# Second FFN of a gated two-layer block: the expert weights of gate and up become the stationary operand, and the second product follows one tile behind

## What is computed

```python
router_logits = jnp.einsum('sbh,eh->sbe', hidden_states, router_w)
routing_indices = jnp.argmax(router_logits, axis=-1)
out = jnp.zeros_like(hidden_states)
for e in range(E):                                   # E = 8, I = 352, H = 128
    mask = (routing_indices == e)[..., None]
    xe = jnp.where(mask, hidden_states, 0.0)
    g = jnp.einsum('sbh,ih->sbi', xe, gate_w[e])
    u = jnp.einsum('sbh,ih->sbi', xe, up_w[e])
    ye = jnp.einsum('sbi,hi->sbh', jax.nn.silu(g) * u, down_w[e])
    out = out + jnp.where(mask, ye, 0.0)
...
x = x + jnp.tanh(g_ffn[1]) * _L1_ffn_ref(_layernorm(x, axis=-1), ...)
```

## Time and profile before

| what | value |
| --- | --- |
| median of 3 runs | 825.99 us (825.89 to 826.08) |
| span of the profiled execution, first to last instruction | 815.2 us |
| around the span (median less span) | 10.8 us |
| mean granted TensorE clock | 0.995 |
| PE busy over the span | 775.3 us, 95% |
| PEld, DVE, ACT, POOL busy | 78%, 76%, 68%, 58% |
| second FFN, from its first instructions to the end of the span | 717.8 to 815.2 us |
| its first products of steps 1 to 12 begin | 729.13 us (step 1) to 797.46 us (step 12) |

### The profile page before, as it was taken

The page is one execution under the profiler, slowest core; times in us unless marked ns, Lnnn a source line. Parts: engine busy times, 40 slices in busy tenths (PEclk is TensorE's granted clock), DMA queues, the critical chain, the costliest instruction groups (busy, mean ns, idle before and its releaser), DMA issues. The chain is left out here.

```text
span 815.2 us, 30741 instructions
## 1 busy us (share of the span) xinstructions
PE 775.3 (95%) x10664; PEld 637.5 (78%) x10669; DVE 622.4 (76%) x2406; ACT 558.0 (68%) x1125; POOL 476.5 (58%) x892
## 2 busy tenths in 40 slices
PE   4999999999999989999999999999999999889995
PEld 2777877787788868888888888888888888558884
DVE  4799999998677767888888888888888888734442
ACT  1688878886455568777777777777777777447762
POOL 6645777773011156577677686676776776605554
PEclk9999999999999999999999999999999999999998
DMA  8804999800200000000000000000000000023110
GB/s 223 303 3 149 264 241 235 195 1 3 72 1 0 0 1 2 3 7 7 7 0 7 7 7 7 7 0 7 7 7 7 0 7 7 10 68 91 33 33 19
DMA packets 56157, 41.65 MB, mean 51 GB/s; under 512 B 3897, under 2 KB 51651, under 8 KB 55856
## 3 DMA queue, kind: packets, MB, share of 16 engines
q1 hardware_dynamic: 52400, 36.39, 17.8%
q0 software_dynamic: 2272, 4.27, 1.6%
q10 hardware_dynamic: 1440, 0.40, 0.4%
HBM read 18.07 MB, written 23.44 MB: 51 GB/s over the span
## 5 line engine op out<-in xcount | busy, mean ns | idle before, releaser
L1654 PE MATMUL l_pv<-l_Z,l_probs 128*128 128x129 f32 x1024 | 164.1, 284 | 0.6 <-DVE l_acc L1161 0.6
L1654 PEld LDWEIGHTS l_pv<-l_Z,l_probs 128*128 128x128 f32 x1024 | 138.4, 191 | 20.0 <-DVE l_acc L1161 4.9
L1433 POOL TENSOR_TENSOR l_qk_lo<-w,l_qk_hi 128x512 f16<-128x512 f32 x132 | 148.9, 1160 | 1.7 <-ACT l_qk_hi L1511 1.3
L1161 DVE SCALAR_TENSOR_TENSOR x_sb<-l_pv,l_inv,x_sb 128x128 f32 (+1 forms) x256 | 89.8, 351 | 35.3 <-DVE l_inv L1148 6.9
L52 PE MATMUL l_tz<-M,cT 128*128 128x512 f16 x396 | 108.0, 382 | 0.2 <-DVE l_Z L1239 0.2
L1497 ACT ACTIVATE l_probs<-l_b 128x512 f32<-128x512 f32 x128 | 72.8, 594 | 50.5 <-PE l_b L1620 50.4
L1487 ACT ACTIVATE w<-l_qk_bank 128x512 f32<-128x512 f32 x129 | 77.0, 597 | 44.1 <-PE l_qk_bank L52 42.4
L520 DVE TENSOR_REDUCE n_shared<-fold_bank 128x4 f32<-128x512 f32 x128 | 87.3, 682 | 9.5 <-PE fold_bank L735 9.3
L1138 DVE TENSOR_REDUCE l_neg_max<-l_a 128x4 f32<-128x512 f32 x132 | 85.8, 681 | 2.6 <-PE l_a L1598 2.1
L1491 ACT ACTIVATE l_qk_hi<-w 128x512 f16<-128x512 f32 x129 | 80.5, 624 | 1.1
L1502 ACT ACTIVATE l_Z<-l_tz 128x512 f32<-128x512 f32 x128 | 76.7, 599 | 3.6
(11 more groups left out here) (291 smaller groups left out, 2266.4 us busy)
## 6 DMA issues: line engine op xcount, KB each, us to landing
expert_rows<-empty_row SPq DMA_DIRECT2D x8, 2178.0 KB, 24.6
x_sb<-expert_rows SPq DMA_DIRECT2D x36, 66.0 KB, 2.1
x_sb<-in_x SPq DMA_DIRECT2D x4, 512.0 KB, 6.9
ctx_sb<-in_ctx SPq DMA_DIRECT2D x4, 512.0 KB, 8.0
w<-in_L_ffn_w SPq DMA_DIRECT2D x1, 2048.0 KB, 9.2
w_raw<-in_L_ffn_gate_w SPq DMA_DIRECT2D x1, 1408.0 KB, 9.6
w_raw<-in_L_ffn_up_w SPq DMA_DIRECT2D x1, 1408.0 KB, 12.2
downT<-in_L_ffn_down_w SPq DMA_DIRECT2D x2, 512.0 KB, 4.3
```

What stands on the lines that cost most here:

```text
L1161: nc.vector.scalar_tensor_tensor(out=total, in0=O[:, h, 0:P], scalar=inv[:, j:j + 1], in1=total, op0=ALU.mult, op1=ALU.add).then_inc(summe ...
L1433: nc.gpsimd.tensor_tensor(qk_lo[:, w, m, Q * u:Q * u + Q].rearrange("p t n -> p (t n)"), qk[:, u, m, :], qk_hi[:, w, m, Q * u:Q * u + Q].r ...
L1654: last = nc.tensor.matmul(pv_bank[m % 2][:, h * (P + 1):(h + 1) * (P + 1)], probs[:, 2 * m + h, :], Z[:, w, 2 * m + h, :], start=True, sto ...
```

## The change

`first_products` swaps the operands. A slice of the expert's weights, 128 (or, for the last chunk, 96) columns wide, is stationary, and the tile's 128 tokens move. Each of gate and up is now three chunks of three matmuls, and a product comes out transposed: up to 128 hidden columns on the partitions, 128 tokens along the bank, three chunks side by side (384 wide). `hid` is therefore already in the form that the second product needs: `transpose_hidden`, the copy to `hidT` and their two semaphores are gone, silu and the multiply are 384 wide instead of 352, and the four banks of gate and up have their unused corner zeroed once. The second product of tile n-1 follows the first products of tile n directly (before, that of n-2), alternates between two output banks, and waits for the result of two tiles ago, where it waited for that of the tile before. The `keep_awake` of step 0 issues 4 matmuls, not 8.

```diff
@@ -1749,20 +1749,19 @@
-        silu = sb("silu", [P, 2, I1])
-        hid = sb("hid", [P, 2, I1])
-        hidT = sb("hidT", [P, 2, WIDE])
+        silu = sb("silu", [P, 2, WIDE])
+        hid = sb("hid", [P, 2, WIDE])
         result = sb("result", [P, 2, U, P])
         taker = sb("taker", [P, 2])
         token = sb("token", [P, 2, U], mybir.dt.uint32)
 
-        t_bank, out_bank, *bank = [ctx.enter_context(nc.psum_tensor(f"f1_bank{n}", [P, 512], F32)) for n in range(8)]
-        gate_bank, up_bank, hT_bank = bank[0:2], bank[2:4], bank[4:6]
-        first_bank = (t_bank, *hT_bank)
+        t_bank, side_bank, *bank = [ctx.enter_context(nc.psum_tensor(f"f1_bank{n}", [P, 512], F32)) for n in range(8)]
+        gate_bank, up_bank, out_bank = bank[0:2], bank[2:4], bank[4:6]
...
@@ -1786,7 +1785,7 @@
 
             @block.vector
             def _(dve):
-                for t in hT_bank:
+                for t in (*gate_bank, *up_bank):
                     nc.vector.memset(t[LAST:P, 2 * P:3 * P], 0.0).then_inc(zeroed, 1)
                 def transposed_lo(i, p):
                     dve.wait_ge(T_hi_ready, U * i + U)
@@ -1799,15 +1798,15 @@
                 def hidden(i, v, w):
                     dve.wait_ge(up_done, U * i + v + 1)
                     dve.wait_ge(silu_ready, U * i + v + 1)
-                    nc.vector.tensor_tensor(hid[:, w, :], up_bank[w][:, 0:I1], silu[:, w, :], ALU.mult).then_inc(hid_ready, 1)
-
-                def results(i, v, half_i, p):
+                    nc.vector.tensor_tensor(hid[:, w, :], up_bank[w][:, 0:WIDE], silu[:, w, :], ALU.mult).then_inc(hid_ready, 1)
+
+                def results(i, v, half_i, p, w):
                     if v == 0:
                         if not isinstance(half_i, int) or half_i:
                             dve.wait_ge(stored[p], 16 * U * half_i)
                         nc.vector.tensor_copy(token[:, p, :], rows[:, bass.ds(U * i, U), TOKEN]).then_inc(token_ready, 1)
                     dve.wait_ge(down_done, U * i + v + 1)
-                    nc.vector.scalar_tensor_tensor(out=result[:, p, v, :], in0=out_bank[:, 0:P], scalar=k.tg[:, 3:4],
+                    nc.vector.scalar_tensor_tensor(out=result[:, p, v, :], in0=out_bank[w][:, 0:P], scalar=k.tg[:, 3:4],
                                                    in1=row(U * i + v), op0=ALU.mult, op1=ALU.add).then_inc(result_ready, 1)
 
                 def step(i, half_i, p, live):
...
-                        if v < 2 and live(-1):
-                            results(i - 1, v + 1, half_i - 1 + p, 1 - p)
-                        if v == 2 and live(0):
-                            results(i, 0, half_i, p)
+                        if v == 0 and live(-1):
+                            results(i - 1, U - 1, half_i - 1 + p, 1 - p, (p + v + 1) % 2)
+                        if v and live(0):
+                            results(i, v - 1, half_i, p, (p + v + 1) % 2)
 
                 for v in range(U):
                     first_lo(v)
@@ -1876,19 +1875,13 @@
 
                 def gated(i, v, w):
                     act.wait_ge(gate_done, U * i + v + 1)
-                    nc.scalar.activation(silu[:, w, :], gate_bank[w][:, 0:I1], ACT.Silu).then_inc(silu_ready, 1)
-
-                def hidden_transposed(n, w):
-                    act.wait_ge(hidT_moved, n + 1)
-                    nc.scalar.activation(hidT[:, w, :], hT_bank[w][:, 0:WIDE], ACT.Copy).then_inc(hidT_ready, 1)
+                    nc.scalar.activation(silu[:, w, :], gate_bank[w][:, 0:WIDE], ACT.Silu).then_inc(silu_ready, 1)
 
                 def step(i, half_i, p, live):
                     begins = isinstance(i, int) and i == 0
                     for v in range(U):
                         if live(0):
                             gated(i, v, (p + v) % 2)
-                        if live(0) and not (begins and v == 0) or live(-1) and v == 0:
-                            hidden_transposed(U * i + v - 1, (p + v + 1) % 2)
                         if v == (2 if begins else 0) and live(1):
                             transposed_hi(i + 1, 1 - p)
                         if v == 1 and live(2) and not begins:
@@ -1931,21 +1924,18 @@
                     T = [t[:, p, v * P:v * P + P] for t in (T_hi, T_lo)]
                     w = (p + v) % 2
                     for hi, lo, bank, done in ((k.gate_hi, k.gate_lo, gate_bank, gate_done), (k.up_hi, k.up_lo, up_bank, up_done)):
-                        weights = [t[:, bass.ds(e, 1), :].rearrange("p a n -> p (a n)") for t in (hi, lo)]
-                        both_products(nc, bank[w][:, 0:I1], [(T[0], weights[0]), (T[0], weights[1]), (T[1], weights[0])]).then_inc(done, 1)
-
-                def transpose_hidden(n, w):
+                        for c, (c0, height) in enumerate(CHUNKS):
+                            weights = [t[:, bass.ds(e, 1), c0:c0 + height].rearrange("p a n -> p (a n)") for t in (hi, lo)]
+                            last = both_products(nc, bank[w][0:height, c * P:c * P + P],
+                                                 [(weights[0], T[0]), (weights[1], T[0]), (weights[0], T[1])])
+                        last.then_inc(done, 1)
+
+                def second_product(n, w, e):
                     pe.wait_ge(hid_ready, n + 1)
-                    for c, (c0, height) in enumerate(CHUNKS):
-                        last = nc.tensor.transpose(hT_bank[w][0:height, c * P:c * P + P], hid[:, w, c0:c0 + height], k.ident[:, :])
-                    last.then_inc(hidT_moved, 1)
-
-                def second_product(n, w, e):
-                    pe.wait_ge(hidT_ready, n + 1)
-                    if not isinstance(n, int) or n:
-                        pe.wait_ge(result_ready, n)
+                    if n > 1:
+                        pe.wait_ge(result_ready, n - 1)
                     for c, (_, height) in enumerate(CHUNKS):
-                        last = nc.tensor.matmul(out_bank[:, 0:P], hidT[0:height, w, c * P:c * P + P],
+                        last = nc.tensor.matmul(out_bank[w][:, 0:P], hid[0:height, w, c * P:c * P + P],
                                                 k.downT[0:height, c, bass.ds(e, 1), :].rearrange("p a n -> p (a n)"),
                                                 start=c == 0, stop=c == len(CHUNKS) - 1)
                     last.then_inc(down_done, 1)
@@ -1958,26 +1948,24 @@
                         if live(0):
                             first_products(i, v, p, now[v], v + 1 if begins else U if v == 0 else 0)
                         if begins and v == 1:
-                            keep_awake(nc, k, out_bank, 8)
-                        if live(0) and not (begins and v == 0) or live(-1) and v == 0:
-                            transpose_hidden(n - 1, (p + v + 1) % 2)
+                            keep_awake(nc, k, side_bank, 4)
                         if v == 0 and live(1) and not begins:
                             transpose(i + 1)
-                        if v < 2 and live(-1):
-                            second_product(n - 2, (p + v) % 2, was[v + 1])
-                        if v == 2 and live(0):
-                            second_product(n - 2, (p + v) % 2, now[0])
+                        if v == 0 and live(-1):
+                            second_product(n - 1, (p + v + 1) % 2, was[U - 1])
+                        if v and live(0):
+                            second_product(n - 1, (p + v + 1) % 2, now[v - 1])
                         if v == 2 and begins:
                             transpose(i + 1)
 
                 pe.wait_ge(k.down_landed, 16 * len(CHUNKS))
-                keep_awake(nc, k, out_bank, 4)
+                keep_awake(nc, k, side_bank, 4)
                 pe.wait_ge(k.first_rows[0], 16)
-                keep_awake(nc, k, out_bank, 2)
-                pe.wait_ge(zeroed, 2)
+                keep_awake(nc, k, side_bank, 2)
+                pe.wait_ge(zeroed, 4)
                 for v in range(U):
                     first_transpose(v)
-                    keep_awake(nc, k, out_bank, 1)
+                    keep_awake(nc, k, out_bank[0], 1)
                 every_step(pe, step)
```

More of the change, by code:

```diff
@@ L1757, in second_ffn @@
         token = sb("token", [P, 2, U], mybir.dt.uint32)
-        t_bank, out_bank, *bank = [ctx.enter_context(nc.psum_tensor(f"f1_bank{n}", [P, 512], F32)) for n in range(8)]
-        gate_bank, up_bank, hT_bank = bank[0:2], bank[2:4], bank[4:6]
-        first_bank = (t_bank, *hT_bank)
+        t_bank, side_bank, *bank = [ctx.enter_context(nc.psum_tensor(f"f1_bank{n}", [P, 512], F32)) for n in range(8)]
+        gate_bank, up_bank, out_bank = bank[0:2], bank[2:4], bank[4:6]
+        first_bank = (t_bank, side_bank, out_bank[1])
         names = ("zeroed taker_ready hn_ready T_moved T_hi_ready T_lo_ready gate_done up_done "
-                 "silu_ready hid_ready hidT_moved hidT_ready down_done token_ready result_ready stored_even stored_odd").split()
```

(3 more changed lines are left out.)

## The result

Over six executions each, the changed kernel takes 831.09 us (829.68 to 834.59) and the kernel before 825.94 us (824.17 to 828.72; three of its six are those of the table of before). The ratio is 1.0066, interval 1.0043 to 1.009: slower by 5.15 us, where +9.3 was forecast.

What follows compares the result with a forecast made beforehand. PE was taken to bound the kernel, its sequencer second. Eleven steps +10.3, step 0 +0.4 and the end -1.4 sum to +9.3 us: span 824.5, time 835.3 us, range 829.5 to 841.5.

Steps and rivals of the forecast that it cites:

- The bound: Second FFN, steps 1 to 11: PE's sequencer, hidden by 1.6 us per step before, becomes the bound and PE starves.
- The size of the step: Second FFN: 56 sequencer starts at 0.117 us plus 0.6 us load, 7.15 us for 6.21; +10.3 us over eleven steps.
- upper bound of 0.125: Longest distance assumed between sequencer starts, in us: step 7.6 us, in all +14.3, time 840.3 us.
- Step 0: First step of the second FFN: two tiles' starts take 3.0 us, then four keep_awake matmuls; +0.4 us.
- The end: From step 12's first product on: the result POOL awaits comes after 3.05 us, not 4.35; -1.4 us in all.
- Priced at nothing: ACT's lost copy, wider silu and multiply, POOL's work, two more memsets: covered by idle time, no effect on the time.
- The time around the span: Whole kernel: the median of the runs was taken to stand 10.8 us above the span of 815.2 us.
- The share of PE: Sign, in the steps: PE's busy share falls from 99% to below 90%, with idle time put down to issue.
- The 311 and 234 register instructions: Sign, line 52: 311 ALU_OP and 234 FUSED_REGOPS in PEldq, two per 0.23 to 0.24 us.
- The clock row: Sign of being wrong: PE's granted clock, 1.00 in the steps before the change, leaves 1.00.
- Loads that don't overlap: Rival, first products: weight loads follow each other at 0.10 us, step 7.9 us, time 843 us; chance 0.06.
- A fall of the whole stage: Rival, second FFN: PE's clock falls to 1.2 GHz, its own step 10.8 + 0.6 us, time near 880; chance 0.03.

Runs made afterwards that it cites:

- third profile of the changed kernel: The changed kernel, unedited, run once more beside the kernel before on the same chip: 828.89 us, ratio 1.0173 to the kernel before.
- kernel with chunks: The kernel before, old operand roles and transposes kept, each 352-column product issued as three of 128, 128 and 96: 835.36 us, ratio 1.0245.
- the later series: Both kernels run again unedited, on three different chips: the kernel before 815.51, 814.93 and 814.91 us, the changed kernel 828.41 and 828.89 us.
- one tile in three: The kernel before with each step's middle tile in the changed form, packed expert numbers loaded every second step, two output banks: 811.68 us, ratio 0.9953.

## Why the prediction was right, and where not

**The bound.** Right. The sequencer, second bound before, became the first, and PE starves: shown by the run that takes the register instructions away and the run that puts them into the old kernel.

**The size of the step** is the term that was mis-sized: 7.15 us forecast, 7.53 measured. The count of 56 starts was right, the distance was not: (7.53 - 0.65)/56 = 0.123 us, not 0.117. Most groups of two starts take 0.23 to 0.24 us, 0.118 apiece; to this come single longer pauses, such as the 0.04 us more between the groups at 778.04 and 778.32. Over the eleven steps of the third profile of the changed kernel the 46 distances that lie over 0.04 us above the usual one for their kind of instruction sum up to 3.6 us more than usual, 0.32 us per step, nearly the whole of the 0.38 that the forecast missed. They stand at no fixed place in a step, but they do have a pattern: the largest, 0.13 to 0.16 us, come some 9 us apart, on average every 255 of PE's instructions (matmuls, loads and register instructions), and in the kernel with chunks every 256; smaller ones follow, mostly 1 us or somewhat more apart. Nothing was run to tell what they are. 0.117 came from 1.3 us of one tile, too short a stretch to show them. The same 0.122 to 0.123 came out of three kernels with 54, 56 and 58 starts. The upper bound of 0.125 held.

**Step 0**: +0.8, not +0.4. Its first two tiles took 3.32 us until `keep_awake` (723.44 - 720.12 in the third profile), not 3.0; from the transposes on it ran as before. **The end**: right, -1.3 for -1.4. The result that releases POOL came at 814.27 + 0.35 - 811.55 = 3.07 us after the first product of step 12, 3.05 forecast, and the scatters run as before. **Priced at nothing**: right; ACT, DVE and POOL have more idle time than before, and PE waited for ACT only in the two long steps of the first profile.

**The time around the span** was a wrong reading, of medians beside one span. Without it the sum would have been +9.3 on 817.

**The ratio.** Forecast 1.0113 (range 1.004 to 1.019); 1.0066 in the first result, 1.016 to 1.017 in the later series, all inside the range. The trace explains the later ones (14.0 us in the profile, 14.0 between the medians) and not the first, since the group near 826 left no trace. That the forecast lies between the two, and that the first time fell inside the range of 829.5 to 841.5 us, is partly luck: the base of 826 was 11 us too high for the kernel that the rows show.

**What would show it.** The share of PE did not fall below 90%: 94%, by overlapping records. The prediction knew that a record of 0.22 us is not the pace of the pairs of the earlier trace rows, and did not apply it to the busy share. The idle time is mostly put down to issue, as forecast, but it is little: 3.1 us of PE's 3.4 in steps 3 to 10. The 311 and 234 register instructions and two per 0.23 to 0.24 us came true. Step 1 began 8.6 us after step 0, not 8.2 (7.82 + 0.4). The clock row did leave 1.00, which the prediction named as a sign of being wrong, and the mechanism held all the same.

**The rivals.** Loads that don't overlap are excluded by the 0.055 us at a fixed address and by the third matmul of each group, 0.05 us behind the second, in the changed kernel. The clock did fall, for 3.41 us in two of three executions of the changed kernel. Step 1 was no longer for it, since PE had so little to do; in the kernel with chunks, where PE also has the transposes, the same fall stood in a step that was longer by 0.85 us. A fall of the whole stage, which the rival priced near 880, did not come.

## What to carry to other kernels

Before replacing few wide matmuls by many narrow ones whose address is known only at run time, count what PE's own sequencer must run per tile (register instructions, waits, loads), times 0.12 us, and set it beside PE's time; the views of busy time don't show this bound. When two bounds lie near each other, move only as much work as balances them: with half of the loads, one tile in three gave 0.9953, none 0.9977 and all three 1.0097. And let the sequencer run ahead before a load, with a second buffer where it would wait.

## What the runs showed of the hardware

- A PE that is starved can stand at 94% busy: the records of 128-column matmuls last 0.22 us each, while they begin every 0.05 to 0.16 us. The spacing of starts tells, not the share.
- Register instructions of 0.032 to 0.051 us by their records start every 0.12 us, with a pause of 0.13 to 0.16 us on top about every 255 instructions of PE.
- The clock stood at 0.50 for 3.41 us near the start of the FFN in three of the six profiled executions whose sequencer is the bound (two of the changed kernel, one with chunks), and in none of the other eight. In all three it fell 1.4 to 1.6 us after PE had stood idle for 1.58 us at the start of step 1, waiting for `T_lo`; a wait there of 1.3 to 1.6 us is in the others too, the kernel before included, without a fall. What decides that was not found.
- A load of one number into PE's sequencer costs 0.65 us where the sequencer is the bound, and showed as 0.2 us at PE where the sequencer was ahead.
- A wait in the sequencer's list held the load and the register instructions behind it: 0.9 us after the instruction before it with one output bank, 0.11 us with two.
